# The columns' second gate sum of a two-way GRU scan, moved from VectorE into a TensorE matmul

## The reference

```
def step(h, xg):
    hg = h @ W_hh.T + b_hh
    xr, xz, xn = jnp.split(xg, 3, axis=-1)
    hr, hz, hn = jnp.split(hg, 3, axis=-1)
    r = jax.nn.sigmoid(xr + hr)
    z = jax.nn.sigmoid(xz + hz)
    n = jnp.tanh(xn + r * hn)
    h_new = (1.0 - z) * n + z * h
...
return (right + down + left + up) / 4.0
...
x = x + _L0_conv_ref(_gn(x), ...)
```

## Time and profile before

| what | value |
|---|---|
| median of 3 runs | 2513.44 us (2509.38 to 2516.88) |
| profiled execution, span from first to last instruction | 2510.1 us |
| profiled execution, own device time | not listed apart from the span |
| first and last sigmoid of the scan's r gate (line 655) start at | 169.7 and 2391.2 us |
| busy: TensorE, VectorE, ScalarE, GpSimd | 86%, 80%, 63%, 61% |
| granted TensorE clock, mean | 0.986 |

### The profile page before, as it was taken

One profiled execution on the slowest core, in us unless ns is written; L12 is line 12 of the kernel. 1 busy time (PEld: TensorE's weight loads), 2 busy tenths in 40 slices (PEclk: granted clock), 3 DMA queues, 4 the chain that ended last, 5 costly groups with the idle time before them and its releaser, 6 DMA issues.

```text
span 2510.1 us, 80982 instructions
## 1 busy us (share of the span) xinstructions
PE 2161.1 (86%) x31528; PEld 1480.8 (59%) x31528; DVE 2016.9 (80%) x4982; ACT 1591.1 (63%) x3401; POOL 1531.5 (61%) x2114
## 2 busy tenths in 40 slices
PE   0689899899979999898979999899979999999995
PEld 0345555566546666566547777566657777555574
DVE  8229999777769999787869999888867777888874
ACT  0236666677758877676747778676657888666600
POOL 2016767567767766666756667667666766776610
PEclk9999999999999999999989999999999999999998
DMA  9983332257789996689999898589987565334699
GB/s 360 292 226 97 96 96 79 66 155 211 239 235 236 244 247 176 174 224 263 303 268 237 231 249 208 141 224 262 314 258 172 147 151 132 73 94 94 152 324 367
DMA packets 325724, 509.26 MB, mean 203 GB/s; under 512 B 24928, under 2 KB 140000, under 8 KB 325344
## 3 DMA queue, kind: packets, MB, share of 16 engines
q1 hardware_dynamic: 307296, 478.23, 69.4%
q10 hardware_dynamic: 18048, 25.85, 2.9%
HBM read 352.98 MB, written 151.01 MB: 201 GB/s over the span
## 4 chain that ended last, share of the span: by engine, by line
PE 35%; DVE 24%; ACT 16%; issue 14%; DMA 6%; POOL 3%; SPq 1%; ACTq 0%; DVEq 0%; POOLq 0%
PE bank L855 20%; ACT r L655 8%; DVE r L994 7%; DVE h L1008 7%; ACT z L659 6%; DMA work<-x 4%; PE bank L856 4%; DVE bank L999 3%; PE bank L835 3%; DVE r L989 3%; ACT bank L663 3%; PE bank L953 2%; PE bank L837 2%; POOL hsum L529 1%; DVE bn L981 1%
## 5 line engine op out<-in xcount | busy, mean ns | idle before, releaser
L855 PE MATMUL bank<-h,wh 64*64 64x256 f32 x6144 | 1488.9, 384 | 165.3 <-DVE h L1008 164.4
L835 PE MATMUL bank<-seq,wx 64*64 64x256 f32 x6144 | 1549.8, 385 | 44.0 <-DMA seq<-seq_next 21.3
L837 PE MATMUL bank<-seq,wx 64*64 64x256 f32 x6144 | 1550.2, 385 | 0.3 <-issue 0.3
L856 PE MATMUL bank<-h,wh 64*64 64x256 f32 x6144 | 1490.0, 387 | 0.1
L537 POOL TENSOR_TENSOR v<-z,h 128x256 f32<-128x256 f32 x1024 | 745.7, 729 | 738.6 <-ACT z L659 737.1
L855 PEld LDWEIGHTS bank<-h,wh 64*64 64x64 f32 x6144 | 730.0, 133 | 526.1 <-PE bank L837 367.4
L835 PEld LDWEIGHTS bank<-seq,wx 64*64 64x64 f32 x6144 | 751.8, 133 | 248.4 <-DVE r L994 126.3
L545 POOL TENSOR_TENSOR hsum<-hsum,h 128x256 f32<-128x256 f32 x1024 | 751.2, 734 | 124.3 <-DVE h L1008 107.7
L837 PEld LDWEIGHTS bank<-seq,wx 64*64 64x64 f32 x6144 | 748.0, 133 | 25.0 <-issue 2.2
L856 PEld LDWEIGHTS bank<-h,wh 64*64 64x64 f32 x6144 | 732.7, 133 | 2.3 <-issue 0.6
L989 DVE SCALAR_TENSOR_TENSOR r<-bank,bhh,r 128x256 f32<-128x256 f32 x1024 | 490.2, 479 | 300.7 <-ACT r L655 246.8
(11 more groups left out here) (95 smaller groups left out, 2453.4 us busy)
## 6 DMA issues: line engine op xcount, KB each, us to landing
work<-x SPq DMA_DIRECT2D x384, 384.0 KB, 6.2
out<-work SPq DMA_DIRECT2D x192, 384.0 KB, 4.6
work<-x SPq DMA_DIRECT2D x143, 512.0 KB, 6.9
work<-x SPq DMA_DIRECT2D x286, 128.0 KB, 7.2
work<-x SPq DMA_DIRECT2D x32, 768.0 KB, 6.5
seq_next<-work SPq DMA_DIRECT2D x48, 512.0 KB, 7.2
work<-hsum_last SPq DMA_DIRECT2D x48, 512.0 KB, 6.8
seq<-x SPq DMA_DIRECT2D x17, 512.0 KB, 7.2
```

The source lines that it names most:

```text
L835: pe.matmul(as_pair(ps[LOW, :], c), wx[HIGH, gate, :], px[HIGH], start=start, stop=False, skip_group_check=True)
L837: return pe.matmul(as_pair(ps[HIGH, :], c), wx[LOW, gate, :], px[LOW], start=start, stop=False, skip_group_check=True)
L855: pe.matmul(ps[LOW, 0:N2], wh[LOW, gate, :], state[LOW], start=start, stop=True, skip_group_check=True)
L856: return pe.matmul(ps[HIGH, 0:N2], wh[HIGH, gate, :], state[HIGH], start=start, stop=True, skip_group_check=True)
```

## The change

`t2` of the columns is no longer a VectorE addition. A new function `add_t1` on TensorE multiplies `t1` of the columns (the SBUF tile `r`) by a unit matrix (`ident`, which the units already use) and accumulates it onto the input part of n in `rx_ps[1]`. `gate_n` of the columns then reads that PSUM bank. `x_r` of the columns now waits for `n_ready[1]` of the step before and no longer for `t2_ready[1]`. The rows keep their VectorE addition.

```
             def gate_n(g, t, c):
                 act.wait_ge(t2_ready[c], T * g + t + 1)
-                act.activation(hn_ps[c][:, 0:N2], r[:, c, :], ACT.Tanh, bias=bih[:, 2:3]).then_inc(n_ready[c], 1)
+                before = r[:, 0, :] if c == 0 else rx_ps[1][:, N2:2 * N2]
+                act.activation(hn_ps[c][:, 0:N2], before, ACT.Tanh, bias=bih[:, 2:3]).then_inc(n_ready[c], 1)
...
             def x_r(g, t, c):
                 if T * g + t > 0:
-                    pe.wait_ge(t2_ready[c], T * g + t)
+                    pe.wait_ge(t2_ready[0] if c == 0 else n_ready[1], T * g + t)
                 x_part(rx_ps[c][:, 0:N2], 0, c, t, True)
...
+            def add_t1(g, t):
+
+                pe.wait_ge(t1_ready[1], T * g + t + 1)
+                pe.matmul(rx_ps[1][LOW, N2:2 * N2], ident[LOW, :], r[LOW, 1, :], start=False, stop=True,
+                          skip_group_check=True)
+                pe.matmul(rx_ps[1][HIGH, N2:2 * N2], ident[HIGH, :], r[HIGH, 1, :], start=False, stop=True,
+                          skip_group_check=True).then_inc(t2_ready[1], 1)
...
                     if beside_input:
                         unit_half(g, u, 0)
+                    add_t1(g, t)
                     if t + 1 < T:
                         x_z(g, t + 1, 0)
...
-            def make_t2(g, t, c):
-                dve.wait_ge(t1_ready[c], T * g + t + 1)
-                dve.tensor_tensor(r[:, c, :], rx_ps[c][:, N2:2 * N2], r[:, c, :], ALU.add).then_inc(t2_ready[c], 1)
+            def make_t2(g, t):
+                dve.wait_ge(t1_ready[0], T * g + t + 1)
+                dve.tensor_tensor(r[:, 0, :], rx_ps[0][:, N2:2 * N2], r[:, 0, :], ALU.add).then_inc(t2_ready[0], 1)
...
                     make_u(g, t, 0)
-                    make_t2(g, t, 1)
                     make_h(g, t, 0)
```

More of the change, by code:

```diff
@@ L1032, in scan @@
                     make_t1(g, t, 0)
-                    make_t2(g, t, 0)
+                    make_t2(g, t)
                     if stats:
```

## The result

| what | before | after |
|---|---|---|
| median, runs on the same chip | 2511.9 us (4 runs, 2509.4 to 2516.9) | 2535.1 us (4 runs, 2529.1 to 2539.7) |
| ratio, 95% interval | 1 | 1.0082 (1.006 to 1.0104) |
| span of the profiled execution | 2510.1 us | 2533.1 us |

The changed kernel is slower by 23 us (15 to 26 by the interval). The page says first what was moved: VectorE lost 93 us of work, TensorE got 155 more, and the time went up.

What follows compares the result with a forecast made beforehand. No engine is full; a chain of dependences round the engines binds, 4.13 us a step. Ordinary steps add 22 us and the 40 steps where TensorE ends last 18: 2513 + 40 = 2553 us, range 2506 to 2590.

Steps and rivals of the forecast that it cites:

- the term for the ordinary steps: 439 ordinary steps, each longer by 0.05 us on the new round trip: 22 us more (0 to 53).
- The old trip without the addition, 3.92: Chain round the engines from h0 to the next h0: without the columns' t2, 0.21 us shorter, 3.92 (pair 3: 3.90).
- Rival one: The addition's place in VectorE's queue was the whole cost: faster, 2439 us; chance 0.09.
- The new round trip, 4.18: Trip n1, x_r1, x_n1, h_r1, r1, t1, add_t1, n1: 4.18 us a step, against 4.13 or 4.11 now.
- the low end: New round trip with 0.67 us for every matmul result, that of x_n1 too: 4.09, so no loss.
- come to the same: Unit steps: add_t1 four turns (1.76 us) after h_r1's start, r1 with t1 takes 1.74; same trip length.
- The 40 heavy steps, +18: 24 whole-tile steps and 16 with unit and projection, where TensorE ends last: 0.44 us more each, 18 us (9 to 23).
- the prediction's upper end of 0.57: In the 40 steps where TensorE ends last: a turn with two longer starts, 0.57 us instead of 0.44.
- Costed at nothing: VectorE's 0.33 us in 21 steps with ending statistics, GpSimd and the transfers: no gain or loss.
- The shorter tanh: Tanh reading PSUM saves 0.10 us, ordinary steps 0.05 shorter than now: 2509 us; chance 0.10.
- Strict order in TensorE: TensorE keeps its queue in order: 189 steps with unit_x_half take 4.30 us, total 2579; chance 0.07.
- Nothing changes: Trips come out equal and the 40 steps find slack: 2513 us; chance 0.04.

Runs made afterwards that it cites:

- the third experiment: The kernel before without VectorE's t2 addition for the columns (tanh n1 reads t1, x_r1 waits for t1): 2439.8 us, ratio 0.9712.

## Why the prediction was right, and where its sizes were off

The forecast was slower by 40 us, the result 23, inside the range. The heavy steps carry it; the term for the ordinary steps was mis-sized, 22 where the traces show 4 to 7, and in pair 0 it had the wrong sign. Point by point:

**The old trip without the addition, 3.92.** Right: 3.93 when nothing takes its place. Rival one, that this is the whole cost, is the 73 us of the third experiment; it falls because a trip of 4.09 replaces the one of 4.13. The margin is narrow: the prediction let this rival decide from 4.07 down.

**The new round trip, 4.18.** The mechanism was right, term for term: `h_r1` hangs on `x_n1`, that on the tanh. What failed is the size of the sum, above all the term "`x_n1` complete, to `h_r1`: 0.72". It came from a tile's end, not the only matmul that waits for another's result (`h_r` waits for `x_n` in every step) but one where that wait ended last; here it is 0.66 (304.39 to 305.05), near the 0.67 that I had kept for the low end. The row was no fixed price even for its own place: in the changed kernel, where `add_t1` stands between the two straight sides, the same tile's end takes 0.68.

```profile
568.02 0.38 PE L767 MATMUL bank<-work,wb 64*64 64x256 f32 x1
...
568.70 0.43 PE L777 MATMUL bank<-work,wa 64*64 64x256 f32 x1
```

What makes this difference was not tried. The tanh with its release was put at 0.53 and is 0.50; 0.02 of that is the shorter tanh below. The others came out within 0.01: 0.49, 0.70, 0.51, 0.54 and 0.69 (the row of `h_r0` reads 0.68, 301.06 to 301.74, for the 0.69 of the sum). Together 4.09, the lower end of the trip that I had worked out, so the steps of pair 0 with statistics gained 0.04 instead of losing 0.05.

**Steps with a unit "come to the same".** They come to 4.14 to 4.16, and by the other branch: `add_t1` stands 1.86 behind `h_r1` (2011.64 to 2013.50), for which I had reckoned four turns of 0.44. They took 0.49, 0.43, 0.45 and 0.49, and that is later than `r1` and `t1` would allow (0.70, 0.51 and 0.54, 1.75). From there the trip goes on as above: `n1` 0.64 later, at 2014.14, `x_r1` 0.50, `x_n1` 0.49 and `h_r1` 0.66 behind, at 2015.79, in all 4.15. Over all ordinary steps the term of +22 us measured +4, or +7 with the single long waits taken out.

**The 40 heavy steps, +18.** Measured +16, or +19 with the single long waits taken out, of which 15 come back when the sum returns to VectorE. Whole-tile steps grew by 0.44 in pair 0 and 0.53 in pairs 1 and 2, the others by 0.58 (medians). Why more than one turn of 0.44 in the last two was not tried; the prediction's upper end of 0.57 was nearer there.

**Costed at nothing.** The 21 steps with ending statistics sum to 111.2 us before and 110.0 after, and GpSimd is as busy as before (1531.5 and 1530.2), so nothing speaks against the zero. Two parts of the change that could have had a price of their own were tried apart: neither the later wait of `x_r1` nor a turn nobody waits for makes the kernel slower by what can be told.

**The shorter tanh.** Partly there: reading PSUM, the tanh takes 448 ns, from SBUF 471 (the page's groups of its line: busy, mean ns of one).

```profile
L664 ACT ACTIVATE bank<-r,bih 128x256 f32<-128x256 f32 x512 | 241.3, 471 | 10.5 <-DVE r L1004 10.3
...
L664 ACT ACTIVATE bank<-bank,bih 128x256 f32<-128x256 f32 x512 | 229.5, 448 | 162.6 <-PE bank L874 162.6
```

23 ns a step, a quarter of the 0.10 that this rival needed. The Trainium skill, page "Perfetto Trace Analysis", section "Optimizing Scalar/DVE Operations", has PSUM cheaper for ScalarE, about 51 ns of overhead for about 93: the trace agrees in direction and not in size, 23 ns apart for 42.

**Strict order in TensorE.** It falls. In the unit step of pair 3, `h_z1` starts at 2012.56, ahead of `x_r0` at 2012.75, which stands before it in the queue, behind the crossed turns of the unit:

```profile
2012.56 0.40 PE L856 MATMUL bank<-h,wh 64*64 64x256 f32 x1
...
2012.75 0.38 PE L838 MATMUL bank<-seq,wx 64*64 64x256 f32 x1
```

and these steps take 4.15, not the 4.30 that it gave.

**Nothing changes.** It was close for ordinary steps (4.160 and 4.169 on average) and falls by the heavy ones and by the measured interval.

## What to carry to other kernels

When an operation goes to another engine, list what its result releases: here the reader of a buffer became a later one, and the buffer's own trip (read, overwrite, complete, use) took the place of the trip that was shortened; with a second buffer where one was free, the kernel became faster than both. Price such a trip from rows of steps that are as loaded as the one in question, since a wait for a matmul's result measured 0.72, 0.68 and 0.66 in three surroundings, and 0.06 times 439 steps is 26 us, more than this term's own size. And before a turn is moved in an engine's queue, ask what fills the queue while it waits: with a unit side in that gap the steps were 0.2 to 0.4 us shorter.

## What was not expected of the hardware

A tanh that reads PSUM and writes PSUM takes 448 ns, one that reads SBUF and writes PSUM 471, at the same 128x256 float32, over 512 of each. A unit-matrix turn takes 0.69 from its start to the tanh that reads the sum (302.71 to 303.40), about the same as from a state part to its sigmoid, so an addition through TensorE came 0.24 later than VectorE's 0.42 plus 0.03; right behind another straight turn it took 0.64 (2013.50 to 2014.14). The share of busy time didn't tell the room on TensorE: at 86% it took another turn in 292 of the 512 steps, and the time moved by 1.7 us, which can't be told from nothing; what seems to bind it in the steps with a unit, once the other trips are cut, is one pair of quarters, and that was only read.
